# A windowed scatter of graph edges on TensorE: the carry between batches as an identity matmul, one register load a batch, and key one-hots of 120 columns

## The chip, the cores and the metric

The kernel runs on one core of one Trainium2 chip. The metric is the device time of one launch in microseconds; the lower the better. In the traces PE is TensorE's matmuls, PEld its weight loads, DVE VectorE, ACT ScalarE, POOL GpSimd and SP the engine whose queue issues most transfers. A name with a q behind it (PEldq, SPq) is that engine's sequencer, which runs register instructions and hands the others on.

## The reference

A graph of 3125 nodes (256 features) and 50000 weighted edges is normalised, propagated three times, and goes through a mixture of 16 experts:

```python
h = x; acc = x                              # x: layernorm of the input
for _ in range(3):
    msgs = vals[:, None] * h[col]
    h = jax.ops.segment_sum(msgs, row, num_segments=n_nodes)
    h = h / max(norm(h), EPS); acc = acc + h
x = x + acc / 4
x = x + moe_ffn(layernorm(x))               # top 2 of 16 experts, layernorm at its end
```

The edges come sorted by the column that the kernel uses as its row order; that is what the windows below rest on.

## The kernel before

The program has six stages behind one another, each a block with a barrier at its end: tables, build, rounds, route, experts, combine. The change touches the tables a little and the build stage above all. The build stage turns the list of edges into a dense matrix `a_rows` in memory, which the rounds then multiply with.

The edges lie in 391 tiles of 128. A window is 6 rows of the matrix. A step pairs one tile with one window; there are 912 steps, in 76 batches of B = 12. For a step the kernel makes, out of table rows `marks`, a one-hot `key_hot` of the edge's place within the window (120 = 6 x 20 places; M in the code, padded to P = 128 before) and a one-hot `lo_hot` over 160 columns (LO). The edge's weight is split in three bf16 parts, and `key_w` is `key_hot` times each part. TensorE multiplies `key_w` (as weights) with `lo_hot` (160 columns): 36 matmuls a batch, 12 steps by 3 parts. Each step adds to the place in PSUM (`ps_w`) of its own window; which of the 12 slots that is comes from the table `place`, loaded into registers.

The engines of the build stage, each with a loop of four batches a turn (batches 8 to 71; the first eight and the last four are written out; VectorE's loop runs from batch 4 on):

- VectorE (`one_hots`, `weigh`): `key_hot` and `lo_hot`, two and a half of the three products `key_w`. It waits for `multiplied` of two batches earlier, since the one-hots are double-buffered. Then, two batches later, `same` and `carry`: the last window of a batch goes on in the next one, so the slot of the batch before at which this one starts is added to its slot 0 in `win`, times `same_b`, which is 1 or 0. The slot is a register, loaded from the table `slot` at each turn of the loop (`slots_of`, 4 values).
- ScalarE: `third`, six products of the third part; then `evacuate` of the batch before, four copies of 480 columns from `ps_w` to `win`, which has a ring of 4 buffers.
- TensorE (`multiply`): on even batches it loads the 24 places of two batches into registers; four matmuls of 2 columns set the start flag of each bank (all 8 banks were cleared once with 512 columns each); then it waits for `hot_ready` and `third_ready` and issues the 36 matmuls. `multiplied` counts up at the last.
- SP (`store`): loads the batch's first window `base` into a register, waits for `carried` and issues four transfers of 12 windows each, every one behind the same part of the batch before, because windows overlap.

Of the kernel before, what the change touches and what calls it, by code (L numbers as in the profile page):

```python
# [20 lines left out]
BF16 = mybir.dt.bfloat16  # L21
# [6 lines left out]
P = 128  # L28
# [61 lines left out]
def phase_tables(nc, s, x, src, dst, ew, hf, tab):  # L90
    with ExitStack() as ctx:
# [85 lines left out]
        def _(pool):  # L177
# [7 lines left out]
            g.iota(tab.key_tab[:, 0:M, :], pattern=[[1, M], [0, 2]], base=0, channel_multiplier=0, **kw)  # L185
            g.memset(tab.key_tab[:, M:P, :], -2.0)
# [29 lines left out]
        def _(dve):  # L216
# [42 lines left out]
            first = tile_of[:].rearrange("p (b j) -> p b j", j=B)  # L259
            v.memset(tab.same[:, 0:1], 0.0)  # L260
            v.tensor_tensor(tab.same[:, 1:s.NB], first[:, 1:s.NB, 0], first[:, 0:s.NB - 1, B - 1], ALU.subtract)
# [26 lines left out]
            link(v.tensor_scalar(moved[:], moved[:], float(B - 1), float(s.LO), ALU.min, ALU.mult))  # L288
            v.tensor_copy(tab.slot[:], moved[:])
# [6 lines left out]
            link(v.tensor_copy(tab.place[:], bank[:]))  # L296
# [34 lines left out]
def phase_build(nc, s, tab, a_dram):  # L331


    with ExitStack() as ctx:
# [14 lines left out]
        key_hot = sb("key_hot", [P, 2, PAIRS, P, 2], BF16)  # L349
        key_w = sb("key_w", [P, 2, 3, PAIRS, P, 2], BF16)  # L350
        zeros = sb("zeros", [P, s.HI * LO])
        same_b = sb("same_b", [P, 2])
        third_b = sb("third_b", [P, 2, B])
        none = sb("none", [P, 512], BF16)
        win = sb("win", [P, RING, B * LO])
# [3 lines left out]
        same_read = sem("same_read")  # L359
# [6 lines left out]
        carried = sem("carried")  # L366
# [27 lines left out]
        def _(sp):  # L394
# [5 lines left out]
            def store(b, i):  # L400
                base = sp.value_load(tab.base[0:1, one(b)], min_val=0, max_val=s.W - 1)
                sp.wait_ge(carried, b + 1)
                for n, part in enumerate(PARTS):
                    if late(b, 1):
                        sp.wait_ge(stored[n], b * 16)
                    sp.dma_start(a_dram[bass.DynSlice(base, B), part, :].rearrange("i p l -> p i l"),
                                 win[part, i, :].rearrange("p (i l) -> p i l", l=LO)).then_inc(stored[n], 16)
# [7 lines left out]
        @block.gpsimd  # L415
        def _(pool):
            g = nc.gpsimd
            g.memset(none[:], 0.0).then_inc(tabs, 1)
            g.memset(zeros[:], 0.0).then_inc(tabs, 1)
            g.memset(win[:, RING - 1, :], 0.0).then_inc(tabs, 1)  # L420

        @block.scalar
        def _(act):
# [12 lines left out]
            def evacuate(b, i):  # L436
                if late(b, RING):
                    act.wait_ge(carried, b - 2)
                    for done in stored:
                        act.wait_ge(done, (b - 3) * 16)  # L440
                act.wait_ge(tabs, 3)
# [15 lines left out]
        def _(dve):  # L457
# [17 lines left out]
            def weigh(b, u, k):  # L475
# [3 lines left out]
                v.tensor_tensor(key_w[:, u, k, 0:n, :, :], key_hot[:, u, 0:n, :, :], mark(b, 2 + k, P)[:, 0:n, :, :],  # L479
                                ALU.mult).then_inc(hot_ready, 1)  # L480

            def same(b, u):

                if late(b, 2):
                    dve.wait_ge(carried, b - 1)
# [1256 lines left out]
```

## Time and profile before

| | |
|---|---|
| median of 3 runs | 1608.08 us (1603.89 to 1608.5) |
| profiled execution, its own time | 1605.87 us |
| its span in the trace | 1604.1 us |
| busy: PE, PEld, DVE, ACT, POOL | 1259.8, 1135.5, 1137.9, 875.4, 209.8 us |
| granted TensorE clock, mean | 0.878 |

The span is cut by the stages. The tables take the first 49 us, the build stage runs from there to 465.3 us, and the rounds start with the reads of `a_rows`. As the stages have barriers between them, what the build stage saves or loses goes into the time one to one unless a later stage changes. The change in the build stage must therefore be read from that stage's own waits and not from the shares over the whole span.

### The profile page before, as it was taken

The page shows a single profiled execution, that of the slowest core. Times are in us where ns is not written, and L with a number is a line of the kernel's source. Part 1 is how long each engine was busy: PE and PEld are TensorE (multiplying, and loading weights), DVE is VectorE, ACT ScalarE, POOL GpSimd, SP SyncE. Part 2 cuts the span into 40 slices and gives each one's busy share as a digit, 9 for nine tenths or more (in the row PEclk, how much of TensorE's full clock was granted, in tenths as well). Part 3 has the DMA queues.
Part 4 walks back from the last instruction along what each step waited for, and adds up shares of the span by engine and source line. Part 5 has one row for each costly group of instructions (what it writes and reads, how often), then busy time and mean ns, then how long its engine had stood idle before and what let it go on. Part 6 is the DMA issues. An engine that isn't in the chain of part 4 may idle for free. (4 is left out here: it accounts for less than half of the span.)

```text
span 1604.1 us, 31106 instructions
## 1 busy us (share of the span) xinstructions
PE 1259.8 (79%) x9152; PEld 1135.5 (71%) x9153; DVE 1137.9 (71%) x2074; ACT 875.4 (55%) x1933; POOL 209.8 (13%) x199
## 2 busy tenths in 40 slices
PE   4467666667648999999999999999754799999600
PEld 1366666666647888888888888888652699999600
DVE  8788888888837656656555766655567498898557
ACT  2577777777735555655545655555321466666312
POOL 1300000000000000000000000000080434444273
PEclk8788887888879999999999999999955799999955
DMA  3187777677787666656666666666222587334373
GB/s 95 45 206 189 181 178 173 166 173 174 182 235 209 183 187 185 182 166 178 187 194 183 187 166 186 176 195 183 88 95 70 188 269 235 109 103 110 118 232 113
DMA packets 228741, 267.64 MB, mean 167 GB/s; under 512 B 16053, under 2 KB 172348, under 8 KB 228582
## 3 DMA queue, kind: packets, MB, share of 16 engines
q1 hardware_dynamic: 205392, 234.01, 52.5%
q0 software_dynamic: 6624, 16.90, 3.9%
q10 hardware_dynamic: 16640, 15.73, 3.2%
q8 instruction: 36, 0.59, 0.1%
q14 instruction: 49, 0.40, 0.1%
HBM read 175.51 MB, written 91.07 MB: 166 GB/s over the span
## 5 line engine op out<-in xcount | busy, mean ns | idle before, releaser
L865 PE MATMUL ps_rows<-h_both,a_high 128*128 (+1 forms) x1875 | 509.7, 400 | 29.4 <-DVE a_low L745 24.1
L745 DVE TENSOR_TENSOR a_low<-a_raw,a_high 128x640 fp32r<-128x640 f32 x375 | 305.8, 823 | 239.0 <-ACT a_high L675 236.0
L675 ACT ACTIVATE a_high<-a_raw 128x640 fp32r<-128x640 f32 x375 | 274.6, 740 | 297.2 <-PE ps_rows L868 283.5
L865 PEld LDWEIGHTS ps_rows<-h_both,a_high 128*128 128x128 f32 x1875 | 332.7, 192 | 87.7 <-issue 24.5
L868 PEld LDWEIGHTS ps_rows<-h_both,a_low 128*128 128x128 f32 x1875 | 277.4, 191 | 33.2
L868 PE MATMUL ps_rows<-h_both,a_low 128*128 (+1 forms) x1875 | 285.7, 283 | 0.0
L558 PE MATMUL ps_w<-lo_hot,key_w 128*128 128x160 bf16 x2736 | 258.5, 264 | 33.1 <-DVE key_w L479 31.0
L558 PEld LDWEIGHTS ps_w<-lo_hot,key_w 128*128 128x128 bf16 x2736 | 243.4, 112 | 37.7 <-issue 35.9
L444 ACT ACTIVATE win<-ps_w 128x480 f32<-128x480 f32 x304 | 147.3, 567 | 71.5 <-PE ps_w L558 57.6
L479 DVE TENSOR_TENSOR key_w<-key_hot,tab_marks 128x1536 bf16<-128x1536 bf16 (+1 forms) x228 | 178.2, 814 | 0.0
L433 ACT ACTIVATE key_w<-key_hot,third_b 128x128 bf16<-128x128 bf16 x456 | 144.5, 426 | 38.2 <-DVE key_hot L470 36.9
L1353 POOL DMA_INDIRECT x_t<-tokens,r_token x80 | 104.4, 1305 | 131.5 <-PE ps_x L1480 118.7
L1367 ACT ACTIVATE w_high<-w_raw 128x1024 fp32r x80 | 80.4, 1052 | 63.1 <-PE ps_o L1512 53.6
L470 DVE TENSOR_TENSOR key_hot<-key_tab,tab_marks 128x1536 bf16<-128x1536 bf16 x76 | 72.3, 951 | 58.6 <-PE ps_w L558 31.2
L1425 DVE TENSOR_TENSOR w_low<-w_raw,w_high 128x1024 fp32r<-128x1024 f32 x80 | 94.4, 1220 | 17.6 <-ACT w_high L1367 12.9
L1495 PE MATMUL ps_h<-x_high,w_high 128*128 128x256 f32 x320 | 94.8, 296 | 0.0
L1011 POOL MEMSET all_ones<- 128x800 f32 x1 | 0.8, 764 | 699.5 <-POOLq L572 699.5
L1495 PE MATMUL ps_h<-x_low,w_high 128*128 128x256 f32 x320 | 91.4, 286 | 0.0
L1495 PE MATMUL ps_h<-x_high,w_low 128*128 128x256 f32 x320 | 91.4, 286 | 0.0
L1512 PE MATMUL ps_o<-w_high,hid_high 128*128 128x256 f32 x320 | 90.0, 281 | 1.3 <-DVE hid_low L1440 1.3
L552 PE MATMUL ps_w<-none 128*128 128x2 bf16 x304 | 18.9, 166 | 91.3 <-issue 91.3
L1512 PE MATMUL ps_o<-w_low,hid_high 128*128 128x256 f32 x320 | 90.1, 281 | 0.0
(225 smaller groups left out, 1576.0 us busy)
## 6 DMA issues: line engine op xcount, KB each, us to landing
a_raw<-a_rows SPq DMA_DIRECT2D x375, 320.0 KB, 3.1
a_rows<-win SPq DMA_DIRECT2D x228, 240.0 KB, 3.6
w_raw<-in_L_ffn_w SPq DMA_DIRECT2D x32, 512.0 KB, 5.0
a_rows<-win SPq DMA_DIRECT2D x76, 180.0 KB
results_sorted<-y_t ACTq DMA_DIRECT2D x40, 256.0 KB, 3.2
b_t<-in_L_ffn_b ACTq DMA_DIRECT2D x40, 128.0 KB, 3.6
hf<-in_x SPq DMA_DIRECT2D x1, 3072.0 KB
x<-in_x SPq DMA_DIRECT2D x1, 3072.0 KB
```

The costliest lines, as they stand in the source:

```text
L433: nc.scalar.activation(key_w[:, u, 2, j // 2, :, j % 2], key_hot[:, u, j // 2, :, j % 2], ACT.Copy, scale=third_b[:, u, j:j + 1]).then_inc ...
L444: ins = nc.scalar.activation(win[:, i, bank * WIDE:(bank + 1) * WIDE], ps_w[:, i % 2, bank * 512:bank * 512 + WIDE], ACT.Copy)
L479: v.tensor_tensor(key_w[:, u, k, 0:n, :, :], key_hot[:, u, 0:n, :, :], mark(b, 2 + k, P)[:, 0:n, :, :], ALU.mult).then_inc(hot_ready, 1)
L558: ins = mm(ps_w[:, u, bass.DynSlice(places[u * B + j], LO)], key_w[:, u, k, j // 2, :, j % 2], lo_hot[:, u, j // 2, :, j % 2], start=False ...
L675: a.activation(a_high[:, u, :], a_raw[:, u, :], ACT.Copy).then_inc(high_split, 1)
L745: v.tensor_tensor(a_low[:, u, :], a_raw[:, u, :], a_high[:, u, :].bitcast(F32), ALU.subtract).then_inc(low_split, 1)
L865: nc.tensor.matmul(ps[:, banks[w][r], :], a_high[:, u, r * P:(r + 1) * P], both, start=first, stop=False, skip_group_check=True)
L868: ins = nc.tensor.matmul(ps[:, banks[w][r], 0:D], a_low[:, u, r * P:(r + 1) * P], upper, start=False, stop=last, skip_group_check=True)
L1353: g.indirect_dma_start(out=x_t[:, t % 2, h, :], out_offset=None, in_=y_dram, in_offset=bass.IndirectOffsetOnAxis(ap=routes.token[:, t * HA ...
L1425: v.tensor_tensor(w_low[n][:, u, :], of_expert(w_raw[n], e), w_high[n][:, u, :].bitcast(F32), ALU.subtract).then_inc(w_low_ready[n], 1)
L1495: ins = mm(ps_h[:, u, f, :], w[0][:, u, at], x[:, u, k, :], start=(n == 0), stop=(n == 3 * KD - 1))
L1512: ins = mm(ps_o[:, u, half, :], h[:, u, f, tokens], w[1][:, u, at], start=(n == 0), stop=(n == 3 * KF - 1))
```

## The change

The carry leaves VectorE. TensorE does it at the end of a batch as one matmul more: an identity `ident` (f32, 128 columns of weights) times 160 columns of the `win` buffer of the batch before, added to slot 0 of `ps_w`. To switch it off where the next batch doesn't continue the window, `win` gets a 13th slot of zeros, and the register that picks the slot may point there. Its value is the 13th entry of `place`, so TensorE loads 13 values each batch in place of 24 every other batch. Since a slot may now be untouched by the 36 matmuls, all 4 banks are cleared with 512 columns in each batch, ahead of the register load. `store` and `evacuate` wait for `evacuated` and for nothing of `carried`, which is gone. `key_hot` and `key_w` have 120 columns in place of 128, for VectorE, ScalarE and as TensorE's weights. VectorE has no register load and no wait for `tabs` left.

```diff
             def store(b, i):
                 base = sp.value_load(tab.base[0:1, one(b)], min_val=0, max_val=s.W - 1)
-                sp.wait_ge(carried, b + 1)
+                sp.wait_ge(evacuated, b + 1)
...
             g.memset(zeros[:], 0.0).then_inc(tabs, 1)
-            g.memset(win[:, RING - 1, :], 0.0).then_inc(tabs, 1)
+            g.memset(win[:, :, B * LO:(B + 1) * LO], 0.0).then_inc(tabs, 1)
+            g.memset(ones[:], 1.0).then_inc(tabs, 1)
+            pool.wait_ge(tabs, 4)
+            g.affine_select(out=ident[:], in_=ones[:], pattern=[[1, P]], compare_op=ALU.is_equal,
+                            fill=0.0, base=0, channel_multiplier=-1).then_inc(tabs, 1)
...
                 if late(b, RING):
-                    act.wait_ge(carried, b - 2)
...
-                v.tensor_tensor(key_hot[:, u, :, :, :], tab.key_tab[:].unsqueeze(1).broadcast_to([P, PAIRS, P, 2]),
-                                mark(b, 0, P), ALU.is_equal).then_inc(key_ready, 1)
+                v.tensor_tensor(key_hot[:, u, :, :, :], tab.key_tab[:].unsqueeze(1).broadcast_to([P, PAIRS, M, 2]),
+                                mark(b, 0, M), ALU.is_equal).then_inc(key_ready, 1)
...
-            def carry(b, i, slot):
...
-                v.scalar_tensor_tensor(win[:, i, start], win[:, (i - 1) % RING, there], same_b[:, i % 2:i % 2 + 1],
-                                       win[:, i, start], ALU.mult, ALU.add).then_inc(carried, 1)
...
             def multiply(b, i):
                 u = i % 2
                 if late(b, 2):
                     pe.wait_ge(evacuated, b - 1)
-                if u == 0:
...
                 for bank in range(BANKS):
-                    mm(ps_w[:, u, bank * 512:bank * 512 + 2], none[:, 0:P], none[:, 0:2],
+                    mm(ps_w[:, u, bank * 512:(bank + 1) * 512], none[:, 0:P], none[:, :],
                        start=True, stop=False, skip_group_check=True)
+                values = nc.values_load_multi_w_load_instructions(
+                    tab.place[0:1, one(b), :].rearrange("p b j -> p (b j)"), engines=[mybir.EngineType.PE], min_val=0,
...
-                        ins = mm(ps_w[:, u, bass.DynSlice(places[u * B + j], LO)], key_w[:, u, k, j // 2, :, j % 2],
+                        ins = mm(ps_w[0:M, u, bass.DynSlice(places[j], LO)], key_w[:, u, k, j // 2, :, j % 2],
                                  lo_hot[:, u, j // 2, :, j % 2],
                                  start=False, stop=False, skip_group_check=True)
+                if late(b, 1):
+                    pe.wait_ge(evacuated, b)
+                    ins = mm(ps_w[:, u, bass.DynSlice(places[0], LO)], ident[:, :],
+                             win[:, (i - 1) % RING, bass.DynSlice(slot, LO)],
+                             start=False, stop=False, skip_group_check=True)
                 ins.then_inc(multiplied, 1)
```

Two places show what stands where on the engines. The first is TensorE at the seam between two batches: the last matmuls of one and the first of the next. Before, the seam ahead of an even batch looks like this (it is the one at the loop's entry; the seam ahead of an odd batch has no load):

```order
L558 MATMUL ps_w<-lo_hot,key_w 128x160 x3
L387 UNCONDITIONAL_BRANCH
L387 ISA
L547 ISA [waits evacuated]
L547 TENSOR_LOAD tab_place
L552 MATMUL ps_w<-none 128x2 x4
L554 ISA
L555 REGISTER_ALU [waits hot_ready_b]
L558 ISA [waits third_ready]
L558 MATMUL ps_w<-lo_hot,key_w 128x160 x3
```

After, every seam of the loop looks like this:

```order
L510 MATMUL ps_w<-lo_hot,key_w 120x160 x3
L515 ISA [waits evacuated]
L515 MATMUL ps_w<-win,ident_c 128x160
L497 MATMUL ps_w<-none 128x512 [waits evacuated]
L497 MATMUL ps_w<-none 128x512 x3
L499 ISA
L499 TENSOR_LOAD tab_place
L506 ISA
L507 REGISTER_ALU [waits hot_ready_b]
L510 ISA [waits third_ready]
L510 MATMUL ps_w<-lo_hot,key_w 120x160 x3
```

The carry with its wait and four wide matmuls now stand ahead of the load, so the array has them to work on while the registers are filled; and the load stands at every seam.

On VectorE, one batch of the loop. Before:

```order
L470 TENSOR_TENSOR key_hot<-key_tab,tab_marks 128x1536
L472 ISA
L472 TENSOR_TENSOR lo_hot<-lo_tab,tab_marks 128x1920
L478 REGISTER_ALU
L479 ISA [waits key_hot_ready]
L479 TENSOR_TENSOR key_w<-key_hot,tab_marks 128x1536
L486 ISA [waits carried]
L486 COPY same_b<-tab_same 128x1
L479 ISA [waits key_hot_ready]
L479 TENSOR_TENSOR key_w<-key_hot,tab_marks 128x768
L504 ISA [waits carried,same_read,evacuated]
L504 SCALAR_TENSOR_TENSOR win<-win,same_b 128x160
```

After:

```order
L467 TENSOR_TENSOR key_hot<-key_tab,tab_marks 128x1440
L469 ISA
L469 TENSOR_TENSOR lo_hot<-lo_tab,tab_marks 128x1920
L475 REGISTER_ALU
L476 ISA [waits key_hot_ready]
L476 TENSOR_TENSOR key_w<-key_hot,tab_marks 128x1440
L476 ISA [waits key_hot_ready]
L476 TENSOR_TENSOR key_w<-key_hot,tab_marks 128x720
```

Two instructions and their three waits are gone from each batch, and four of the five that stay have 120 columns a step in place of 128.

## Rows read from the trace of the kernel before

**Rows 1.** The stretch 78 to 450 us: busy of each engine, clock, DMA share, GB/s.
```profile
78.00:450.00 372.00, 255.85 (x2863) 245.63 (x2862) 321.64 (x499) 274.32 (x782) 0.00 (x0) 0.83 0.75 180
```
**Rows 2.** Waits of PE and of DVE, 88 to 450 us: sum, times, longest.
```profile
PE ps_w L552 <- issue: 90.4, 35, 4.2
DVE key_hot L470 <- PE ps_w L558: 31.2, 14, 3.8
```
**Rows 3.** Timeline of PE over one turn: start, us, and idle time before.
```profile
398.40 2.75 PE L558 MATMUL ps_w<-lo_hot,key_w 128*128 128x160 bf16 x36 [1.67 <-DVE key_w L479]
...
404.33 4.98 PE L558 MATMUL ps_w<-lo_hot,key_w 128*128 128x160 bf16 x36
...
418.60 2.75 PE L558 MATMUL ps_w<-lo_hot,key_w 128*128 128x160 bf16 x36 [1.40 <-DVE key_w L479]
424.39 0.25 PE L552 MATMUL ps_w<-none 128*128 128x2 bf16 x4 [3.04 <-issue]
```
**Rows 4.** Register loads by line and stretch: count, ns min/median/max, first and last start.
```profile
L547 PEldq TENSOR_LOAD <-tab_place x35: 1952/3375/4654, 84.1 to 440.3; - x35
...
L547 PEldq TENSOR_LOAD <-tab_place x2: 1622/1627/1632, 65.1 to 73.8; - x2
...
L547 PEldq TENSOR_LOAD <-tab_place x1: 3987/3987/3987, 400.0 to 400.0; - x1
...
L491 DVEq TENSOR_LOAD <-tab_slot x18: 1504/2314/3541, 91.5 to 447.6; - x18
...
L401 SPq TENSOR_LOAD <-tab_base x14: 479/692/1094, 78.5 to 137.4; - x14
```
**Rows 5.** Timeline of DVE over one batch and the next one's start.
```profile
434.43 0.95 DVE L470 TENSOR_TENSOR key_hot<-key_tab,tab_marks 128x1536 bf16<-128x1536 bf16 x1
435.30 1.15 DVE L472 TENSOR_TENSOR lo_hot<-lo_tab,tab_marks 128x1920 bf16<-128x1920 bf16 x1
436.36 1.81 DVE L479 TENSOR_TENSOR key_w<-key_hot,tab_marks 128x1536 bf16<-128x1536 bf16 x2
...
438.16 0.54 DVE L479 TENSOR_TENSOR key_w<-key_hot,tab_marks 128x768 bf16<-128x768 bf16 x1
438.63 0.37 DVE L504 SCALAR_TENSOR_TENSOR win<-win,same_b 128x160 f32<-128x160 f32 x1
438.93 0.94 DVE L470 TENSOR_TENSOR key_hot<-key_tab,tab_marks 128x1536 bf16<-128x1536 bf16 x1
```
**Rows 6.** Weight loads: 414.3 to 416.9, 476.9 to 477.5, 470 to 472 us.
```profile
L558 PEld LDWEIGHTS ps_w<-lo_hot,key_w 128*128 128x128 bf16 x36 | 2.5, 97 | 0.2 <-issue 0.2
...
L868 PEld LDWEIGHTS ps_rows<-h_both,a_low 128*128 128x128 f32 x5 | 0.7, 189 | 0.1
...
L865 PEld LDWEIGHTS ps_rows<-h_both,a_high 128*128 128x128 f32 x5 | 1.5, 322 | 19.4 <-issue 19.1
```
**Rows 7.** Five f32 matmuls of 256 columns (timeline), and two stretches' granted clock.
```profile
477.00 0.76 PE L868 MATMUL ps_rows<-h_both,a_low 128*128 128x256 f32 x5
...
470.00:472.00 2.00, 1.96 (x5) 1.58 (x6) 1.26 (x4) 1.00 (x3) 0.00 (x0) 0.50 0.95 340
476.90:480.00 3.10, 3.10 (x20) 2.75 (x19) 0.00 (x0) 0.00 (x0) 0.00 (x0) 1.00 1.10 349
```
**Rows 8.** The route stage's f32 matmuls with 128 columns, at half clock.
```profile
L1191 PE MATMUL ps_y<-ident,hf x50: 417/421/473, 1176.1 to 1207.1; 128*128 128x128 f32 x50
```
**Rows 9.** The page's row of the four stores: count, KB each, us to landing.
```profile
a_rows<-win SPq DMA_DIRECT2D x228, 240.0 KB, 3.6
```
**Rows 10.** Timeline at the build stage's start and end.
```profile
54.27 3.60 PE L536 MATMUL ps_w<-none 128*128 128x512 bf16 x8 [16.32 <-POOL win L420]
...
59.45 2.75 PE L558 MATMUL ps_w<-lo_hot,key_w 128*128 128x160 bf16 x36 [1.50 <-DVE key_w L479]
...
448.39 2.74 PE L558 MATMUL ps_w<-lo_hot,key_w 128*128 128x160 bf16 x36
...
465.27 0.31 POOL L662 MEMSET x<- 128x256 f32 x1 [411.06 <-POOLq L334]
```

More of the change, by code:

```diff
@@ L365, in phase_build @@
         evacuated = sem("evacuated")
-        carried = sem("carried")
         padded = sem("padded")
@@ L488, in slots_of @@
-            def slots_of(b, n):
-                at = slice(b, b + n) if isinstance(b, int) else bass.DynSlice(b, n)
-                _, values = nc.values_load_multi_w_load_instructions(
-                    tab.slot[0:1, at], engines=[mybir.EngineType.DVE], min_val=0, max_val=(B - 1) * LO,
-                    skip_runtime_bounds_check_because="a slot is LO times the minimum with B - 1 of a count")
-                return values
-            def carry(b, i, slot):
-                there = bass.DynSlice(slot, LO)
-                start = slice(0, LO)
-                dve.wait_ge(evacuated, b + 1)
-                dve.wait_ge(same_read, b + 1)
-                if late(b, 1):
-                    dve.wait_ge(carried, b)
-                v.scalar_tensor_tensor(win[:, i, start], win[:, (i - 1) % RING, there], same_b[:, i % 2:i % 2 + 1],
-                                       win[:, i, start], ALU.mult, ALU.add).then_inc(carried, 1)
@@ L507, in run @@
-            def run(b, i, slot):
+            def run(b, i):
                 u = i % 2
                 one_hots(b, u)
-                weigh(b, u, 0)
-                weigh(b, u, 1)
-                if late(b, 2):
-                    same(b - 2, u)
-                weigh(b, u, 2)
-                if late(b, 2):
-                    carry(b - 2, (i - 2) % RING, slot)
-            dve.wait_ge(tabs, 3)
-            slots = slots_of(0, 2)
-            for b in range(RING):
-                run(b, b, slots[b - 2] if b >= 2 else None)
@@ L522, in _ @@
-            with dve.Fori(1, NB // RING) as it:
-                slots = slots_of(it * RING - 2, RING)
-                for i in range(RING):
-                    run(it * RING + i, i, slots[i])
-            slots = slots_of(NB - 2, 2)
-            for b in (NB - 2, NB - 1):
-                same(b, b % 2)
-                carry(b, b % RING, slots[b - (NB - 2)])
+                for k in range(3):
+                    weigh(b, u, k)
+            batches(dve, run)
         @block.tensor
@@ L533, in _ @@
             mm = nc.tensor.matmul
-            pe.wait_ge(tabs, 3)
-            for bank in range(2 * BANKS):
-                mm(ps_w[:, bank // BANKS, bank % BANKS * 512:(bank % BANKS + 1) * 512], none[:, 0:P], none[:, :],
-                   start=True, stop=True, skip_group_check=True)
-            places = []
+            pe.wait_ge(tabs, 5)
             def multiply(b, i):
```

47 lines of the change are left out of this document (18 added, 29 removed).

## The prediction

> **What bounds the kernel now.** Only the build stage changes, and a barrier ends it, so I read that stage alone: first its busy shares, then its waits, then one turn of its loop. Over 372 us of it VectorE is busy 321.6 us (86%), ScalarE 274.3, TensorE 255.9, and the transfers take 0.75 of the DMA engines' time [rows 1]. VectorE looks like the bound, yet it isn't it alone: its largest wait is for TensorE's last matmul (31.2 us in 14 waits), while TensorE stands idle 90.4 us for "issue" ahead of the first matmul of a batch [rows 2]. "Issue" has a name in the trace: the register load of 24 places runs 3375 ns in the median in this stretch, and 1627 ns in the two loads that fell before the stores began [rows 4]. The load that begins at 400.0 lasts 3.99 us, and the batch behind it starts at 404.33, 0.34 us after its end [rows 3, 4].
>
> The turn then reads so [rows 3, 5]. VectorE needs 4.50 us a batch (434.43 to 438.93). Two of its batches, 9.0 us, bring TensorE to an odd batch (418.60), which takes 2.75 us; the load leaves the array idle for 3.04 us; the even batch then takes 4.98 us, because the clock has fallen in the idle time; only its end lets VectorE start the batch after next. 9.0 + 2.75 + 3.04 + 0.3 + 4.98 = 20.1 us for four batches. From 398.40 to 418.60, one turn, are 20.2 us. Over the whole stage the first batch's matmuls end at 62.20 and the 76th's at 451.13 [rows 10]: 388.9/75 = 5.19 us a batch.
>
> **VectorE's part.** The carry and `same_b` fall away: from the last `key_w` to the next `key_hot` are 0.77 us (438.16 to 438.93), of which 0.47 is the product itself (to 438.63) and 0.30 the carry; the small copy costs 0.06 in its place. The shorter one-hots: 384 elements more make 1.15 of 0.95 us, 0.52 ns an element; so 96 less in three instructions and 48 less in one save 0.05 + 0.05 + 0.05 + 0.025 = 0.17 us. 4.50 - 0.36 - 0.17 = 3.97 us a batch [rows 5]. Its own register load (2.3 us a turn, rows 4 in L491) goes too. VectorE then has 0.9 us of slack to what follows.
>
> **TensorE's part.** This becomes the bound, with a cycle of its own at each seam. Its terms:
> - The 36 matmuls: 2.75 us at full clock, if 120 columns of weights cost no more than 128 do. Below, the other case.
> - The sequencer runs ahead of the array. The load at 400.0 begins 1.15 us before the array's end (398.40 + 2.75) [rows 3, 4]. The carry and four clears now stand ahead of the load, five more pairs in the queue; at the 0.07 us at which 36 matmuls follow each other I add 0.35.
> - The load of 13 values, under traffic. Between SP's one value (692 ns) and PE's 24 (3375 ns) a straight line gives 2.1 us; with the 3987 ns of the load whose neighbours I read, 2.4; from VectorE's four values (2314) to PE's 24, 2.8 [rows 4]. Below, 1.6 us, the quiet load of 24; above, 3.4, if the count didn't matter. I take 2.4, because stores will run almost without a pause.
> - 0.34 us from the load's end to the first matmul.
> - 0.25 us for the loop's branch, once in four, and for jitter: no row, an allowance.
>
> The seam is -1.15 + 0.35 + 2.4 + 0.34 = 1.95 us. The cycle is 2.75 + 1.95 + 0.25 = 4.95, say 4.9 us.
>
> The carry matmul and the clears lie inside that seam. Eight clears of 512 columns took 3.60 us at the slow clock [rows 10], 0.43 each, half of it at the fast one: four are 0.86. The carry is an f32 matmul; the nearest, with 128 columns, took 421 ns at half clock [rows 8]; I take 0.45 us, with 0.25 and 0.9 as the ends. 1.3 us of array work beside a seam of 1.95: hidden, with 0.6 to spare. Were the load free, it would be the seam. The carry's wait for `evacuated` of the batch before is hidden as well: ScalarE starts to copy when that batch ends and needs some 2 us, while the carry comes 1.95 + 2.75 = 4.7 us after it. Behind that wait stand the clears and the next load, so it would hurt if ScalarE were late; at 274.3 us over 372 it isn't [rows 1]. Array work of about 4 in 4.9 us, with no gap over 1 us, keeps the clock at its upper level of 2.4 GHz, and the even batches' 4.98 us become 2.75.
>
> **Stores.** SP's register load begins once a batch; its starts run from 78.5 to 137.4 us, 14 of them, 4.53 us apart [rows 4], in a stretch in which the stores were issued back to back. I take 4.53 us as their floor; 4.9 lies above it. The stores begin no earlier than before, at about 74 us, since they wait for the padding's transfer.
>
> **Start and end.** Before, DVE and PE waited for a memset of `win`; VectorE may now start at once; TensorE still waits for GpSimd until about 54 us, and its four slow clears (1.7 us) stand ahead of the first batch, which so ends near 58 instead of 62.20 us. 58 + 75 x 4.9 = 425.5. Then copies (2 us), one store (4.53) and its landing (3.6) [rows 9]: 10.1, where before 14.1 us passed from 451.13 to 465.27 [rows 10], with a store or so still queued. 435.6 against 465.3: 29.7 us less. From 1605.9 of the profiled execution that is 1576 us. The runs' median is 1608.1, 2.2 above it; I say 1577.
>
> **A rule of the skill that speaks against the change.** What rows show first. A weight load of 128 bf16 columns is 97 ns long, and matmuls of 160 columns follow each other every 0.07 us; one of 128 f32 columns is 189 ns long at a granted clock of 1.00 and 322 ns at 0.50 [rows 6, 7]. Five f32 matmuls of 256 columns take 0.76 us, so with 0.28 for the last 0.12 apart [rows 7], hence weights of 128 f32 columns come at least every 120 ns. If 120 bf16 columns come no faster, 36 matmuls are 113 ns apart, 35 x 0.113 + 0.23 = 4.2 us; if time goes by bytes, 56 ns and hidden. The f32 load is shorter at the higher clock, so it isn't bound by something that stands still, and bf16 has half its bytes: I take the lower. The Trainium skill, "TensorE: Matmul & The Clock Gate", section "Weight-path perf modes — Fast Weight Load (FWL) and DoubleRow", says that the fast weight load is on only where there are 128 weight columns and the type isn't FP32; its section "LDWEIGHTS (loading the stationary operand)" puts the plain load at columns / 1.2 ns, 100 ns for 120 columns. By that page an estimate of the block is 3.7 us, of the cycle 5.5, and of the time 1619 us.
>
> **The rivals.**
> - Weights slower (chance 0.20). Place: the 36 matmuls. With 113 ns between them the block grows by 1.45 us; the sequencer's lead, some 16 matmuls (1.15/0.07), grows to 1.8, which gives 0.65 back. 4.9 + 0.8 = 5.7 us; 58 + 427.5 + 10 = 495.6, 30 us more: 1636 us. It decides where the spacing passes about 95 ns (cycle 5.3). For it: whole-row f32 loads are twice as long. Against it: that they follow the clock.
> - The load is as dear for 13 values as for 24 (0.10). VectorE's four values at 2.3 us speak for it, SP's one at 0.7 and the quiet loads against. Cycle 4.9 + 1.0 = 5.9; 1650 us. It decides at a load of 2.9 us.
> - The stores' floor holds (0.15): the load needs under 2.0 us, the cycle wants less than 4.53. 74 + 76 x 4.53 + 3.6 = 422: 43 us less, 1563 us.
> - Nothing is gained (0.05): TensorE's clock or ScalarE's turn eats it, cycle 5.3, about 1606 us.
> - The forecast (0.50): cycle 4.7 to 5.1, 1562 to 1592 us.
>
> **How the numbers follow.** The time is the forecast's. A measurement of this kernel tells 0.3%, 5 us, from no change. Faster: 0.50 + 0.15, and a little of the cases at the edge: 0.67. Slower: 0.20 + 0.10 less those edges: 0.27. Same: 0.06. The range is to leave out 2 in 10: below the floor's 1560 lie 0.05, above 1630 the dear load and half of the slow weights. 1560 to 1630; the forecast's own is 1562 to 1592.
>
> **What would show it.** The spacing of the 36 matmuls (0.07 or 0.10 and more) and the weight load's length; the length of a 13-value load (2.4); the granted clock in the stage (0.83 before, near 1.00 after); DVE batches of 3.97 us with waits for TensorE between them; starts of SP's loads 4.9 apart; the rounds' start near 436 us. The prediction is wrong if the matmuls are 0.10 apart, if the load ends later than the clears by over 1.5 us, or if the carry's wait shows as TensorE's idle time.

## The result

The changed kernel is slower: 1840.69 us in the median of four runs (1839.02 to 1845.02), beside 1608.29 us for the kernel before on the same chip; ratio 1.1456, 95% interval [1.1428, 1.1484]. The forecast was 1577 us, with 1560 to 1630 as its range. Nearly the whole difference of 232 us lies where the prediction looked: the rounds start at 692.26 us, where 465.27 was before [rows 10] and 435.6 was forecast, so 227 us are the build stage's. Some of the kernels below have two groups of executions some 25 us apart (e12 has four from 1577.7 to 1580.72 us and two at 1603.53 and 1605.83), and a ratio leaves the longer ones out.

### The profile page after: what moved, and what is told of

It is laid out like the page before. It is cut to its first block and busy times, and to the rows that moved or that the text cites. A ratio compares the mean times of both kernels' runs of the same rounds, so it can differ in the third digit from the quotient of the medians.

```text
span 1837.3 us, 30941 instructions
## 1 busy us (share of the span) xinstructions
PE 1369.6 (75%) x9294; PEld 1201.7 (65%) x9295; DVE 1100.6 (60%) x1920; ACT 877.1 (48%) x1933; POOL 212.3 (12%) x200
## 5 line engine op out<-in xcount | busy, mean ns | idle before, releaser
L510 PE MATMUL ps_w<-lo_hot,key_w 128*120 128x160 bf16 x2736 | 287.9, 280 | 246.1 <-issue 236.7
L510 PEld LDWEIGHTS ps_w<-lo_hot,key_w 128*120 128x120 bf16 x2736 | 275.7, 170 | 279.0 <-issue 275.8
L467 DVE TENSOR_TENSOR key_hot<-key_tab,tab_marks 128x1440 bf16<-128x1440 bf16 x76 | 68.9, 907 | 317.8 <-PE ps_w L515 311.3
L476 DVE TENSOR_TENSOR key_w<-key_hot,tab_marks 128x1440 bf16<-128x1440 bf16 (+1 forms) x228 | 164.5, 777 | 0.0
L432 ACT ACTIVATE key_w<-key_hot,third_b 128x120 bf16<-128x120 bf16 x456 | 141.2, 418 | 5.3 <-DVE key_hot L467 2.9
L497 PE MATMUL ps_w<-none 128*128 128x512 bf16 x304 | 81.3, 391 | 16.5 <-POOL ident_c L418 16.5
L1469 PE MATMUL ps_o<-w_high,hid_low 128*128 128x256 f32 x320 | 89.7, 280 | 0.0
```

The lines of the kernel that those rows point to most:

```text
L432: nc.scalar.activation(key_w[:, u, 2, j // 2, :, j % 2], key_hot[:, u, j // 2, :, j % 2], ACT.Copy, scale=third_b[:, u, j:j + 1]).then_inc ...
L510: ins = mm(ps_w[0:M, u, bass.DynSlice(places[j], LO)], key_w[:, u, k, j // 2, :, j % 2], lo_hot[:, u, j // 2, :, j % 2], start=False, stop ...
L1469: ins = mm(ps_o[:, u, half, :], h[:, u, f, tokens], w[1][:, u, at], start=(n == 0), stop=(n == 3 * KF - 1))
```

## The profile after

The page's rows of the slices and of the build stage's largest groups (columns as the page gives them: busy us and mean ns, then idle time before and its releaser):

```profile
PEclk8787777778777878999999999999996569999955
GB/s 83 95 137 99 114 120 96 105 120 116 95 110 121 107 105 238 194 187 185 186 153 187 186 186 186 157 187 185 185 167 39 106 167 267 197 107 105 91 240 115
...
L510 PE MATMUL ps_w<-lo_hot,key_w 128*120 128x160 bf16 x2736 | 287.9, 280 | 246.1 <-issue 236.7
L510 PEld LDWEIGHTS ps_w<-lo_hot,key_w 128*120 128x120 bf16 x2736 | 275.7, 170 | 279.0 <-issue 275.8
```

A slice is 46 us. In the build stage, now slices 2 to 15, the transfers move 95 to 137 GB/s, where 180 was before [rows 1], and the clock stands at 7 to 8 tenths (0.83 before). All but 10 of the 246.1 us for which TensorE idles ahead of these matmuls is "issue". The waits from 88 to 600 us (sum, times, longest) answer to [rows 2]:

```profile
ACT win L441 <- PE ps_w L515: 275.0, 43, 9.7
DVE key_hot L467 <- PE ps_w L515: 271.7, 46, 9.4
...
PE ps_w L510 <- issue: 202.5, 42, 7.4
```

VectorE and ScalarE wait for TensorE half of the time; TensorE waits for "issue", up to 7.4 us at once. SP in its turn waits for ScalarE's copies, all that it waits for in this stretch:

```profile
SPq L401 <- ACT win L441: 225.5, 33, 8.4
```

The timeline of TensorE answers to [rows 3]:

```profile
298.85 2.80 PE L510 MATMUL ps_w<-lo_hot,key_w 128*120 128x160 bf16 x36 [0.26 <-issue]
301.49 0.47 PE L515 MATMUL ps_w<-win,ident_c 128*128 x2
301.80 1.03 PE L497 MATMUL ps_w<-none 128*128 128x512 bf16 x4
309.33 5.05 PE L510 MATMUL ps_w<-lo_hot,key_w 128*120 128x160 bf16 x36 [6.50 <-issue]
314.18 0.73 PE L515 MATMUL ps_w<-win,ident_c 128*128 x2
314.75 1.03 PE L497 MATMUL ps_w<-none 128*128 128x512 bf16 x4
315.62 2.54 PE L510 MATMUL ps_w<-lo_hot,key_w 128*120 128x160 bf16 x33
```

Of two seams one is cheap and one costs 6.50 us of an idle array. What "issue" is, the register loads of 13 values say. All 76 of them first, then five that follow each other (count, ns min/median/max, first and last start):

```profile
L499 PEldq TENSOR_LOAD <-tab_place x76: 1097/3266/9160, 54.2 to 669.4; - x76
...
L499 PEldq TENSOR_LOAD <-tab_place x1: 3104/3104/3104, 295.4 to 295.4; - x1
...
L499 PEldq TENSOR_LOAD <-tab_place x1: 8169/8169/8169, 300.8 to 300.8; - x1
...
L499 PEldq TENSOR_LOAD <-tab_place x1: 1107/1107/1107, 312.7 to 312.7; - x1
L499 PEldq TENSOR_LOAD <-tab_place x1: 8016/8016/8016, 317.5 to 317.5; - x1
...
L499 PEldq TENSOR_LOAD <-tab_place x1: 3102/3102/3102, 329.3 to 329.3; - x1
```

3.1, 8.2, 1.1, 8.0, 3.1: the same instruction, 13 values each time. This cycle of four holds from the tenth load to the last. It has two causes. One is the company, as the windows of the first four loads show (PE, PEld, DVE, ACT, POOL busy, clock, DMA share, GB/s):

```profile
295.40:298.50 3.10, 3.10 (x19) 2.31 (x17) 0.57 (x1) 0.69 (x2) 0.00 (x0) 0.64 0.00 0
300.80:308.90 8.10, 2.03 (x18) 1.26 (x16) 5.25 (x7) 4.87 (x15) 0.00 (x0) 0.94 0.86 205
312.70:313.80 1.10, 1.10 (x11) 1.10 (x10) 0.00 (x0) 0.00 (x0) 0.00 (x0) 0.50 0.00 0
317.50:325.50 8.00, 2.05 (x19) 1.28 (x16) 5.68 (x8) 5.22 (x17) 0.00 (x0) 0.75 0.81 187
```

During the two long loads the stores run, at 0.81 and 0.86 of the DMA engines' time; during the short ones none does. I read it so: a load of 8 us holds TensorE up, the copies and with them the stores run dry (SP's 225.5 us above), so the next load has no company, ends early, and is followed by one beside stores again. The other cause must tell 3.10 from 1.107 us, both without a store. A row of `place` now has 13 values of 4 bytes, 52 bytes: only every fourth batch's row begins at a multiple of 16 bytes. Before, two batches' 96 bytes always did. That is the theory which the experiments test: a register load that begins at a multiple of 16 bytes fetches four values with each read, and any other one value with each read. The same trace has the fourth case as well, rows that begin at a multiple of 16 bytes beside stores, before the cycle sets in: the loads of batches 4 and 8 (counted from 0) take 2.98 and 3.42 us, where their unaligned neighbours take up to 8.7.

```profile
L499 PEldq TENSOR_LOAD <-tab_place x1: 2984/2984/2984, 75.3 to 75.3; - x1
...
L499 PEldq TENSOR_LOAD <-tab_place x1: 3420/3420/3420, 109.8 to 109.8; - x1
```

## The experiments

Each ratio is against the kernel before, run on the same chip and in the same series of runs. That kernel took 1607.42 us beside e1 to e4, 1611.05 beside e5 to e8, and 1623.04 and 1624.33 beside e9 to e12, so times of different series are not compared as they stand. The traces put most of that difference behind the build stage: from the start of the rounds to the end pass 1135 to 1147 us in e1 to e8 and 1152 to 1159 in e9 to e12. So the start of the rounds in each run's trace compares the build stages themselves:

| before | after | e1 | e2 | e3 | e4 | e5 |
|---|---|---|---|---|---|---|
| 465.27 | 692.26 | 456.90 | 712.15 | 443.00 | 451.96 | 466.50 |

| e6 | e7 | e8 | e9 | e10 | e11 | e12 |
|---|---|---|---|---|---|---|
| 455.08 | 421.53 | 481.54 | 428.10 | 433.95 | 708.46 | 424.18 |

**Rows of 16 values** (e1: the changed kernel, rows of 64 bytes):

```diff
-        self.place = sb("tab_place", [1, s.NB, s.BATCH + 1], I32)
+        self.place = sb("tab_place", [1, s.NB, 16], I32)
```

> The changed kernel with one thing different: a batch's 13 places stand 64 bytes apart in their table in place of 52, so that every load begins at a multiple of 16 bytes. Theory A (alignment): a load that begins at a multiple of 16 bytes reads four values at a time, any other reads one value at a time, and each read costs about 0.25 us when no store runs and 0.57 us beside stores. Then all 76 loads need four reads: 1.1 us quiet, about 2.3 beside stores, none near 8, and the time comes near what was predicted for the change, 1560 to 1590 us. Theory B (count): an odd count, 13, is what is dear: loads stay at 3 and 8 us and the time at about 1840. Theory C (company): the wide clears and the f32 carry that now run beside the load slow it down: again 3 to 8 us and about 1840.

Measured: 1602.01 us, ratio 0.9959 [0.9935, 0.9983]: some 240 us less than the changed kernel, from three spare values a row. Its loads (all, those from 78 to 430 us, and one):

```profile
L499 PEldq TENSOR_LOAD <-tab_place x76: 1102/2867/3802, 54.2 to 441.8; - x76
...
L499 PEldq TENSOR_LOAD <-tab_place x67: 1805/2917/3802, 82.6 to 426.8; - x67
...
L499 PEldq TENSOR_LOAD <-tab_place x1: 2917/2917/2917, 305.6 to 305.6; - x1
```

The window 78 to 430 us, columns as above:

```profile
78.00:430.00 352.00, 267.96 (x2780) 218.31 (x2814) 272.35 (x337) 263.96 (x742) 0.00 (x0) 0.99 0.79 184
```

TensorE's timeline around that load:

```profile
303.66 2.81 PE L510 MATMUL ps_w<-lo_hot,key_w 128*120 128x160 bf16 x36 [0.74 <-issue]
306.31 0.47 PE L515 MATMUL ps_w<-win,ident_c 128*128 x2
306.62 1.03 PE L497 MATMUL ps_w<-none 128*128 128x512 bf16 x4
308.88 2.80 PE L510 MATMUL ps_w<-lo_hot,key_w 128*120 128x160 bf16 x36 [1.24 <-issue]
```

No load of 8 us is left, the alternation is gone, and the clock in the stage is 0.99. The load still takes 2.92 us beside stores, not the 2.4 of the prediction nor the 2.3 of the expectation, and the cycle is 5.2 us: the gain ends at 0.4%, and the expected 1560 to 1590 us are missed. Theories B and C are out, since the count and the company stayed as they were.

**The kernel before, off by two values** (e2), the same fault put into a kernel that hadn't got it:

```diff
-                    both = slice(b * B, (b + 2) * B) if isinstance(b, int) else bass.DynSlice(b * B, 2 * B)
+                    both = slice(2 + b * B, 2 + (b + 2) * B) if isinstance(b, int) else bass.DynSlice(b * B + 2, 2 * B)
```

> The kernel before with its table of places moved by two values, 8 bytes, and nothing else: 24 values a load, every other batch, but beginning 8 bytes off a multiple of 16. Theory A: 24 reads in place of 6, so 5.8 us quiet and up to 13.7 beside stores instead of 1.6 and 3.4; with 34 loads in the loop and the stores ending in the meantime some 4 to 8 us more each: 1750 to 1900 us. Theories B and C: nothing of the count or of what runs beside the load changes, 1608 us and 3.4 us a load.

Measured: 1850.7 us, ratio 1.1522 [1.15, 1.1544]. Nothing of the change is in this kernel; only the table's start has moved. Its load of 24 values, 3375 ns before [rows 4]:

```profile
L547 PEldq TENSOR_LOAD <-tab_place x38: 6834/10342/12646, 54.3 to 683.2; - x38
```

Eight bytes off makes the load three times as long.

**Every load off by one value** (e11: the changed kernel, rows of 16 values, the 13 from the second on):

```diff
-                    tab.place[0:1, one(b), :].rearrange("p b j -> p (b j)"), engines=[mybir.EngineType.PE], min_val=0,
+                    tab.place[0:1, one(b), 1:2 + B].rearrange("p b j -> p (b j)"), engines=[mybir.EngineType.PE], min_val=0,
```

> The changed kernel with rows of 16 values, of which the 13 begin at the second, so that every load begins 4 bytes off a multiple of 16. Alignment theory: 13 single reads in every batch, 3.1 us in the quiet and about 7 to 8 beside stores, and no load of 1.1 us as every fourth one of the changed kernel has; slower than the changed kernel's 1840 us, or near it if the stores, being further apart, leave more of each load in the quiet: 1840 to 1950 us. If the row's start did not matter and only its length of 64 bytes did, this is e1: 1602 us.

Measured: 1873.65 us, ratio 1.1552 [1.1521, 1.1583]. The expectation's "7 to 8 beside stores" holds, but I had each load beside stores; in fact they alternate here too, and a quiet one is 3.10 in both places where the changed kernel has 3.1 and 1.1:

```profile
L499 PEldq TENSOR_LOAD <-tab_place x1: 8110/8110/8110, 289.1 to 289.1; - x1
L499 PEldq TENSOR_LOAD <-tab_place x1: 3100/3100/3100, 301.0 to 301.0; - x1
L499 PEldq TENSOR_LOAD <-tab_place x1: 7508/7508/7508, 306.3 to 306.3; - x1
L499 PEldq TENSOR_LOAD <-tab_place x1: 3101/3101/3101, 317.6 to 317.6; - x1
```

With e1 this settles it: the length of a row isn't what matters, its start is.

**VectorE's load aligned** (e4: the kernel before, `slot` shifted by two values, so that its load of four begins at a multiple of 16 bytes; before, it began 8 bytes off):

```diff
-                at = slice(b, b + n) if isinstance(b, int) else bass.DynSlice(b, n)
+                at = slice(b + 2, b + 2 + n) if isinstance(b, int) else bass.DynSlice(b + 2, n)
```

> The kernel before with VectorE's table of slots moved by two values, so that the loop's load of 4 values begins at a multiple of 16 bytes; nothing else. Theory A: one read in place of four, 0.3 to 0.7 us in place of 2.3 a turn; as VectorE at that place waits for TensorE too, at most half of the 1.7 us shows: 0 to 15 us less than 1608. Theories B and C: the load stays at 2.3 us and the time the same.

Measured: 1589.79 us, ratio 0.9902 [0.9884, 0.992], 13 us by the start of the rounds. The load, 2314 ns before [rows 4]:

```profile
L491 DVEq TENSOR_LOAD <-tab_slot x18: 747/964/1357, 90.9 to 435.6; - x18
```

Four values in one read cost 0.96 us beside stores, where SP's one costs 0.69. The first load of the loop, at 72.1 us, falls where no store runs yet; it takes 986 ns in the kernel before and 376 ns here:

```profile
L491 DVEq TENSOR_LOAD <-tab_slot x1: 986/986/986, 72.1 to 72.1; - x1
...
L491 DVEq TENSOR_LOAD <-tab_slot x1: 376/376/376, 72.1 to 72.1; - x1
```

So the rule holds on VectorE's sequencer too, and the kernel before paid for it. The rule has a limit, though. The dearest load here (1357 ns, the last) has only two values, and it also begins at a multiple of 16 bytes. In e10 it is the same, the last load of four values first, then the one of two:

```profile
L490 DVEq TENSOR_LOAD <-tab_slot x1: 537/537/537, 399.3 to 399.3; - x1
...
L490 DVEq TENSOR_LOAD <-tab_slot x1: 1030/1030/1030, 418.7 to 418.7; - x1
```

Two values cost twice what four do. At the stage's start VectorE's first load, of two values, takes 782 ns aligned (before) and 775 ns 8 bytes off (here). So it seems that only full groups of four are fetched at once and the values left over one by one; 13 values, three groups and one value, make four reads by either count.

**Columns alone** (e3: the kernel before, `key_hot` and `key_w` with 120 columns):

```diff
-                v.tensor_tensor(key_hot[:, u, :, :, :], tab.key_tab[:].unsqueeze(1).broadcast_to([P, PAIRS, P, 2]),
+                v.tensor_tensor(key_hot[:, u, :, :, :], tab.key_tab[:].unsqueeze(1).broadcast_to([P, PAIRS, M, 2]),
...
-                        ins = mm(ps_w[:, u, bass.DynSlice(places[u * B + j], LO)], key_w[:, u, k, j // 2, :, j % 2],
+                        ins = mm(ps_w[0:M, u, bass.DynSlice(places[u * B + j], LO)], key_w[:, u, k, j // 2, :, j % 2],
```

> The kernel before with the 120 columns alone, for the one-hots, the products and TensorE's weights. If narrow weights cost nothing: VectorE's batch 4.33 in place of 4.50 us, two of them in each turn's chain, so 0.35 us less in 17 turns: 6 us less, 1602 us, 1598 to 1608. If TensorE's matmuls came 0.1 us apart at full clock (rival of the prediction), 1.1 us more for the odd batch of each turn and none for the slow one: 12 us more.

Measured: 1582.09 us, ratio 0.9855 [0.9835, 0.9876]. This one edit gains 25 us. The expectation had 6, so it missed most of the gain. VectorE's 0.17 us a batch are 6 us if only two batches of a turn wait for it, 13 if all do; VectorE's register load is shorter in this trace as well (median 1400 ns, 2314 before), which would be 0.9 us a turn or up to some 15 us. What shortened it was not tried apart.

**12 values in each batch** (e5: the kernel before, its 24 in two halves):

```diff
-                if u == 0:
-                    both = slice(b * B, (b + 2) * B) if isinstance(b, int) else bass.DynSlice(b * B, 2 * B)
+                if True:
...
-                        tab.place[0:1, both], engines=[mybir.EngineType.PE], min_val=0,
+                        tab.place[0:1, steps(b)], engines=[mybir.EngineType.PE], min_val=0,
```

> The kernel before with one load of 12 places in each batch in place of 24 in every other one; rows of 48 bytes keep every load at a multiple of 16 bytes. Nothing else. Theory A (a read takes four values where the start is a multiple of 16 bytes, 0.25 us quiet and 0.6 to 0.7 beside stores): three reads a batch in place of six every other: 0.8 us quiet, 2.0 beside stores. As the sequencer starts a load about 1 us ahead of the array's end, the idle time is 1 to 1.5 us at each seam in place of 3 at every other, the clock falls less often, and the time is 0 to 25 us less than 1607. Rival: a load has a fixed price beside stores, over 2.9 us, whatever its count: 12 values as dear as 24 and the time 20 to 60 us more. So this run prices the part of the change that loads once a batch, without the alignment.

Measured: 1611.61 us, ratio 0.9992 [0.9967, 1.0017]: no difference that can be told, where up to 25 us less were expected. The load is 2.26 us long, not the 2.9 and more of the rival with a fixed price: the count of reads matters. First where no store runs yet, then from 78 to 430 us:

```profile
L546 PEldq TENSOR_LOAD <-tab_place x5: 848/862/1272, 54.3 to 73.9; - x5
...
L546 PEldq TENSOR_LOAD <-tab_place x67: 1262/2262/2882, 80.1 to 426.6; - x67
```

**Another partition** (e6: e1 with the table on partition 127 in place of 0; for that it is worked out on all partitions):

```diff
-                    tab.place[0:1, one(b), 0:B + 1].rearrange("p b j -> p (b j)"), engines=[mybir.EngineType.PE], min_val=0,
+                    tab.place[127:128, one(b), 0:B + 1].rearrange("p b j -> p (b j)"), engines=[mybir.EngineType.PE], min_val=0,
```

> The changed kernel with rows of 16 values, and its table of places kept and read on partition 127 in place of 0. The stores read partitions 0 to 119 of the window buffer, never 120 to 127. Theory P (place): a register load is slow beside stores because both read the same partition or its neighbours: the load falls from 2.9 us to near 1.1, the cycle from 5.2 to near the stores' floor of 4.5, and the time to 1550 to 1575 us. Theory R (road): the delay lies on the shared way to memory, wherever the table lies: the load stays at 2.9 us and the time at about 1602.

Measured: the load is 2982 ns in the median (2917 in e1) and 1.15 us where no store runs, so in the profiled execution the other partition makes the load no shorter. The ratio, 0.9757 [0.9703, 0.9811], leaves out the longer two of the four executions (1572.47, 1580.46, 1600.3 and 1603.87 us), and the profiled one is the longest; whether the partition helps in the shorter ones is not shown, and I draw nothing from the time. The trace shows something else. Within this one execution, with the same instructions, the loads change their length at about 244 us:

```profile
L499 PEldq TENSOR_LOAD <-tab_place x15: 1442/2203/3088, 175.4 to 238.9; - x15
...
L499 PEldq TENSOR_LOAD <-tab_place x37: 2666/3162/3432, 244.0 to 439.8; - x37
```

The transfers take 0.85 of the DMA engines' time in the stretch of the shorter loads and 0.74 in the other, so it isn't more traffic that makes them longer. How a load falls against the stores seems to count, and it can stay one way or the other for long.

**Without the carry** (e7: e1 less the carry and its wait; the last window of a batch loses what it had before):

```diff
-                if late(b, 1):
-                    pe.wait_ge(evacuated, b)
-                    ins = mm(ps_w[:, u, bass.DynSlice(places[0], LO)], ident[:, :],
-                             win[:, (i - 1) % RING, bass.DynSlice(slot, LO)],
-                             start=False, stop=False, skip_group_check=True)
```

> The changed kernel with rows of 16 values and without the carry: the identity matmul and its wait for evacuated are left out, so sums of a window that goes on across two batches are not joined. If, as predicted, the carry hides inside the seam behind the register load, the time stays within 5 us of 1602. If its wait or its two parts of f32 weights stand on the path, the cycle falls by 0.3 to 0.5 us and the time by 20 to 40 us.

Measured: 1575.11 us (1563.56 to 1588.24), ratio 0.9776 [0.9707, 0.9844], some 29 us less than e1 by the two ratios. The prediction had the carry hidden. What costs in the traces is not the 0.47 us of array work: the load itself is shorter, here in the shortest of the four executions (2917 ns in e1).

```profile
L499 PEldq TENSOR_LOAD <-tab_place x71: 1533/2432/3543, 76.6 to 400.1; - x71
```

**The carry with zeros of bf16** (e12: e1, same number of instructions, same wait, other operands):

```diff
-                    ins = mm(ps_w[:, u, bass.DynSlice(places[0], LO)], ident[:, :],
-                             win[:, (i - 1) % RING, bass.DynSlice(slot, LO)],
+                    ins = mm(ps_w[:, u, bass.DynSlice(places[0], LO)], none[:, 0:P],
+                             none[:, 0:LO],
```

> As e1 (rows of 16 values), but the matmul of the carry takes bf16 zeros for both operands in place of the f32 identity and the window buffer: it adds nothing, so the last window of a batch loses what it had before. Number of instructions, wait and place stay. In e7, without the carry and its wait, the cycle fell from 5.2 to 4.6 us, of which 0.47 was a shorter register load (2.39 for 2.86 us) and 0.12 an earlier one. Theory F: the load is longer because the carry's f32 operands, the 160 columns of the window buffer above all, are read beside it; then the load is 2.4 us here, the cycle near 4.6 to 4.8, and the time near e7's ratio of 0.978. Theory W: what costs is the carry's place in the queue and its wait for the copies, whatever it reads (the load falls at another moment against the stores); then the load is 2.9 us here and the ratio e1's 0.996.

Measured: 1580.09 us, ratio 0.972 [0.9696, 0.9743], worked out from the four executions of 1577.7 to 1580.72 us; two more took 1603.53 and 1605.83. The profiled one is of the four, and its loads are as theory F has them:

```profile
L499 PEldq TENSOR_LOAD <-tab_place x70: 1777/2460/3440, 82.6 to 406.2; - x70
```

So the wait and the place in the queue don't by themselves make the load long. That the f32 operands do is likely but not shown. The load of e6, which has the f32 carry, is 2.2 us long for a stretch of its trace, and two of e6's four executions took 1572.47 and 1580.46 us; e12, without f32 operands, has two of six that are 25 us longer. The rival is that the carry only changes how often the loads fall badly against the stores, and no run keeps the two apart. If it is the operands, it stays open whether their reading costs, or that an f32 product stands in the timeline as two (x2 in the rows at L515 above).

**The clears behind the load** (e8: e1, the four clears moved behind the register load):

```diff
-                for bank in range(BANKS):
-                    mm(ps_w[:, u, bank * 512:(bank + 1) * 512], none[:, 0:P], none[:, :],
...
+                for bank in range(BANKS):
+                    mm(ps_w[:, u, bank * 512:(bank + 1) * 512], none[:, 0:P], none[:, :],
```

> The changed kernel with rows of 16 values and its four wide clears behind the register load in place of ahead of it. If the clears hide behind the load where the change puts them, here they stand on the path: 0.87 us more in each of 76 batches, less what the stores' floor or VectorE give back, 50 to 70 us more than 1602. If the clears weren't hidden before either, the time stays.

Measured: 1629.41 us, ratio 1.0092 [1.0065, 1.0119]. By the two ratios that is some 21 us or 0.28 us a batch over e1, where 50 to 70 us were expected. The place ahead of the load is worth that much of the clears' 1.03 us. It isn't the full price, since the load also begins earlier here, 1.18 us before the block's end in the median where e1 has 0.89.

**Rows of 12 values** (e9: the changed kernel; the place of step 0 is always 0, so its entry can hold the carry's slot):

```diff
-                    skip_runtime_bounds_check_because="it is the place of a slot below B") for place in values[0:B]], values[B]
+                    skip_runtime_bounds_check_because="it is the place of a slot below B") for place in values[1:B]], values[0]
+                at = [slice(0, LO)] + [bass.DynSlice(place, LO) for place in places]
...
-        self.place = sb("tab_place", [1, s.NB, s.BATCH + 1], I32)
+        self.place = sb("tab_place", [1, s.NB, s.BATCH], I32)
```

> The changed kernel, but with 12 values a batch in place of 13: the place of step 0 is always slot 0, so its entry holds the carry's slot, and the rows of 48 bytes all begin at a multiple of 16. Alignment theory: three reads of four values in place of three and a bit (13 aligned values are four reads), so the load is about 0.85 us in the quiet and 2.2 beside stores, as it was in the kernel before with 12 values each batch (2.22), where e1's was 2.9. The seam shrinks by 0.7 us at most; since in e1 VectorE bounds a part of the batches, the cycle goes from 5.2 to some 4.6 to 4.8 us and the time to 1560 to 1575 us, which would beat both kernels. If the load's length beside stores were set by the traffic alone and not by reads, it stays at 2.9 us and the time at 1602.

Measured: 1583.98 us beside 1623.04 for the kernel before, ratio 0.9754 [0.9729, 0.9778]: it beats both kernels (0.9754 of the 1607.42 us of e1's series is 1568, within the expected 1560 to 1575). TensorE's loads from 78 to 430 us, and SP's over the whole stage:

```profile
L499 PEldq TENSOR_LOAD <-tab_place x70: 1018/2076/2817, 83.9 to 402.5; - x70
...
L396 SPq TENSOR_LOAD <-tab_base x76: 467/980/1307, 72.8 to 420.3; - x76
```

All that SP waited for from 88 to 400 us:

```profile
SPq L401 <- DMA a_rows<-win: 1.8, 7, 0.3
```

SP doesn't wait for a copy any more (29.4 us in e1, same stretch), and its batches are 347.5/75 = 4.63 us apart: the stores bound the stage, near the 4.53 us that the prediction gave as their floor.

**Both edits of the kernel before** (e10: e3 and e4 together, with both diffs):

> The kernel before with two of the single edits together: key one-hots and products of 120 columns (alone 1582) and VectorE's load of four values begun at a multiple of 16 bytes (alone 1590). If the two gains are of different things they add: 1608 - 25 - 20 = about 1565 us. If both only let VectorE keep up with the same next bound (TensorE's turn with its load of 24, or the stores' 4.53 us), the second adds little: 1575 to 1582 us.

Measured: 1588.1 us beside the same 1623.04, ratio 0.9788 [0.9768, 0.9808]. They don't add in full (0.9855 times 0.9902 would be 0.976), yet two thirds of the second gain are there. With e9 it shows what is left of the rest of the change (carry on TensorE, wide clears, a load each batch) once every load is aligned: 0.9754 against 0.9788, 4 us in the medians and 6 by the start of the rounds, with intervals that overlap a little.

## Why the prediction was wrong

**The step that failed** is "The load of 13 values, under traffic": 2.4 us, by a straight line over the count of values. The count isn't what a load costs; reads are. Lengths by number of reads, without and beside stores:

| load | reads | quiet, us | beside stores, us |
|---|---|---|---|
| SP, 1 value [rows 4] | 1 | | 0.69 |
| VectorE, 4 aligned (e4, e10) | 1 | 0.38 | 0.96, 0.55 |
| PE, 12 aligned (e5, e9) | 3 | 0.85 | 2.26, 2.08 |
| VectorE, 4 off [rows 4] | 4 | 0.99 | 2.31 |
| PE, 13 aligned (after, e1) | 4 | 1.11 | 2.92 |
| PE, 24 aligned [rows 4] | 6 | 1.63 | 3.38 |
| PE, 13 off (after, e11) | 13 | 3.10 | 8.0 |
| PE, 24 off (e2) | 24 | 6.8, 7.2 | 10.3 |

Quiet, a read costs 0.24 to 0.30 us where there are three or more, 0.38 where there is one. Beside stores it costs 0.56 to 0.75 in the rows with 3 to 13 reads and 0.55 to 0.96 in those with one. In the last row it is 0.43, because those loads outlast the stores: the transfers take 0.57 to 0.59 of the DMA engines' time in three of them, where a load of the changed kernel has 0.81 to 0.86. The rows before had the sign of it: four values took 2314 ns and 24 took 3375. A sixth of the values for two thirds of the time doesn't lie on a line with SP's one at 692, and I used the three as a range in place of asking why. The other bound, 3.4 us "if the count didn't matter", was no bound for the same reason.

**What it did to the turn.** From 298.85 to 315.62 are two batches. The first: the load begins at 300.8, 1.9 us after the block's start, and lasts 8.17; 0.4 later the next block starts. 10.48 us in place of 4.95: 5.53 more, about the load's own error of 8.17 - 2.4 = 5.77. The second: the clock has fallen in the idle time, the block takes 5.05 at half clock, and 1.24 for the seam, whose load is quiet, 6.29 in all. The mean is 8.4 us against the forecast 4.9; over 75 batches 8.2 (first and last load, 54.2 and 669.4), 3.3 more, 248 us of the 257 by which the rounds start later than forecast.

**Point by point.** The cycle of TensorE was the bound: right. The sequencer's lead of 0.8 us before the block's end: 0.9 measured (300.8 against 298.85 + 2.80). Load's end to first matmul 0.34: 0.40. VectorE 3.97 us a batch: 4.06 (key_hot of 302.20 to the last key_w's end at 306.26). The carry's 0.45 us of array: 0.47 at full clock, 0.73 at half. That the carry is hidden: wrong, by some 29 us (e7); in the traces these come through the load's length. That its wait is hidden: right (TensorE waits for the copies there once in e1, for 0.3 us, and e12 keeps the wait). That the clears are hidden: their place ahead of the load gains 0.28 us a batch (e8), and how much of them still shows isn't told. "The clock at its upper level": right once the loads are aligned (0.99 in e1), wrong in the changed kernel, where it stands at 0.50 in the block behind a load of 8 us (312.7 to 313.8 above). The load beside stores is dearer than the 2.4 us even where aligned: 2.92. In e1 the seam behind 303.66 is 308.88 - 306.47 = 2.41 us where the forecast has 1.95, the load's 0.5 more, and the cycle is 5.2, near the 5.3 of the rival "nothing is gained". That rival blamed the clock or ScalarE; the clock is at 0.99, and TensorE waits for ScalarE's products only 9.1 us from 88 to 450 us. The stores' floor: right, and reached by e9.

**The rivals.** The slower weights didn't come. From 299.2 to 301 us in the changed kernel:

```profile
L510 PEld LDWEIGHTS ps_w<-lo_hot,key_w x27: 132/133/135, 299.1 to 301.0; 128*120 128x120 bf16 x27
```

A weight load is 133 ns long, where it was 97 [rows 6]; but the block is 2.80 us against 2.75, so it lies beside other work and costs 2% of the block, and e3 with the same columns is faster. The Trainium skill's rule that the fast weight load wants 128 columns ("TensorE: Matmul & The Clock Gate", section "Weight-path perf modes — Fast Weight Load (FWL) and DoubleRow") points to a longer load, and the trace has one. The Trainium skill's figure for the plain load (same page, "LDWEIGHTS (loading the stationary operand)") makes 100 ns for 120 columns, where the trace has 133. Taken as the spacing of the matmuls, as the prediction's estimate by the Trainium skill took it, it makes a block of 3.7 us, and the trace has 2.80. The rival of a dear load had the right place and the right sign, with a mechanism (length without regard to count) that e5, e9 and e1 contradict and a price of 1650 us that was too low by 190.

## What to carry to other kernels

Lay out a table that is read into registers so that every load begins at a multiple of 16 bytes, and count its cost in reads of four values (a value left over seems to cost a read of its own); rows of 52 bytes in place of 64 cost some 240 us here, and putting the 13th value into an entry that was always 0 brought the load down to three reads. When two rows of one kind of instruction don't fit a line, find what differs before a third is interpolated between them. A matmul of 0.47 us that seems hidden behind a register load can still cost: leaving it out gained 29 us, though by which way is open.

## What was not expected of the hardware

- A register load of 13 values takes 1.11 us where it begins at a multiple of 16 bytes and 3.10 otherwise, with no transfer running; beside stores at 0.8 of the DMA engines' time 2.92 and 8.0. Offsets of 4 (e11) and 8 bytes (the quiet 3.10 of the changed kernel) cost the same. It holds on TensorE's and on VectorE's sequencer. A load of two values costs twice one of four where both begin at a multiple of 16 bytes (1.03 and 0.54 us in e10). With the table on partition 127 the load is no shorter in the execution that was profiled (2.98 us, 2.92 on partition 0).
- Long loads and stores alternate: after a load of 8 us beside stores the next one runs in 1.1 or 3.1 us with no transfer beside it, and this lasts to the stage's end.
- One and the same load can be 2.2 or 3.2 us long for tens of batches within one execution (e6). With the f32 carry ahead of it it was 2.92 us in e1, 2.46 with bf16 operands (e12) and 2.43 without the carry (e7); that the operands are the cause isn't shown.
- Weights of 120 bf16 columns load in 133 ns in place of 97, and the matmuls behind them keep their pace within 2%.
